# An eight-stage network on one core: table lookup of the last feed forward in parts on GpSimd beside five earlier stages, turned maxima in another bank, transposes moved in the 32-wide attentions

## The chip, the cores and the metric

One core of one Trainium2 chip. The metric is the device time of one execution in microseconds. The kernel has four batches of 512 rows of 512 float32 values and eight stages, four attentions and four feed forwards. The engines are named as in the profile: PE is TensorE, DVE is VectorE, ACT is ScalarE, POOL is GpSimd, SP is SyncE.

## What is computed

```
x = L0_attn_x                                  # (4, 512, 512)
x = x + attention(layernorm(x))                # a0: 16 heads of 32, 4 key/value heads, causal
x = x + feed_forward(layernorm(x), scales)     # f0: silu(x g) * (x u) through 1408, scaled
x = x + attention(layernorm(x), biases)        # a1: 16 heads of 32, own layernorm inside
x = x + mixture_of_depths(layernorm(x))        # m1: 64 of 512 rows are chosen
x = x + attention(layernorm(x), rope, biases)  # a2: one head of 512
x = x + ternary_feed_forward(layernorm(x))     # f2
x = x + window_attention(layernorm(x))         # a3: 16 heads of 128, window of 128
# f3: the weights are given as indices into a table of 16 values
gate, up = x @ lut[gate_idx].T, x @ lut[up_idx].T     # 1376 x 512 each
x = x + (silu(gate) * up) @ lut[down_idx].T
```

The indices are int32, laid out by the host as 11 groups of 3 matrices of 128x512 (`f3_idx`). `lut[idx]` must give the exact float32 value.

## The kernel before

Every stage is one `nc.Block` or more, with a program for each engine, and a barrier of all engines at its end: no instruction of a stage starts before all engines have ended the one before. The stages and their stretches of the profiled span are a0 16.5 to 531.0, f0 to 914.6, a1 to 1487.2, m1 in two blocks to 1621.2 and 1930.9, a2 to 2260.4, f2 to 2698.3, a3 to 3568.5 (with a short block to 2770.2 ahead), the table block of f3 to 3840.8, and f3 itself to 4222.0. Activations x stay in SBUF. Nearly every product is done as three matmuls on a high and a low part of both operands (`product`, L95 to L97), so each weight and each activation is split: ACT or POOL makes the high part (`_hi`), DVE or POOL subtracts it (`_lo`).

In the attentions an `ORDER` list, written out in Python, gives the order of work; each engine walks through all of it and does its own share of each entry, waiting on semaphores. PSUM has 8 banks; `jobs` says which job uses which bank, and `vacant`, `full` and `read` are the waits that come with it.

- **attention32** (a0, a1). A batch b has four units u of four heads. "max" computes scores for the row maxima (banks 0 to 2, DVE reduces them in L595), "rows" turns the negated maxima (`L`) on PE (L725) and ACT copies them to `mrow` (L514); "exp" computes transposed scores with the maxima added (banks 3 to 5), ACT does the exponential (L523) into `PT`; "pv" sums, "bc" spreads the reciprocals, DVE multiplies into `OT_raw` (L628), and in a0 POOL splits it (L471, L473). At the end of a batch stand "T" (PE transposes the next batch's xn, ACT evicts, POOL casts in L456, DVE subtracts in L560), "pv" of the last unit, "qkv" of the next batch, and "Y". The turned maxima use bank 0. There are 64 "exp" entries in each stage.
- **feed_forward** (f0, f3). For each batch, 11 chunks j: PE does gate and up of chunk j + 1, then down of chunk j. ACT applies silu, DVE multiplies by up (`sg`), and POOL makes `h_hi` (L1008) and `h_lo` (L1010), for which PE waits before down. In batch 0 ACT and DVE also split the weights, four chunks ahead (L1020, L1075). The next batch is normalised at j = 6 into four `xn` buffers (L1063) and turned on PE (`turn`, L1124) before the last down. SP issues three small loads and 11 weight loads at the start (L977 to L982).
- **the table block of f3** (lines 871 to 933). SP loads the indices, DVE takes the four bits of each index, ACT makes for each of 8 pairs of table values the one that the lowest bit chooses, in the eight banks, and DVE's copy_predicated picks by the other bits, then splits into `W[0]` and `W[1]`. PE and POOL have no work in it. f3 itself then loads and splits nothing.
- **mixture_of_depths** (m1). In its first block POOL does only the roots of each batch (L2296, L2297) between DVE's statistics (L2326, L2329) and DVE's normalisation (L2335); DVE's further chain of a batch follows. SP issues 13 loads, the last four of 2 MB each (L2286).
- **attention512** (a2). POOL multiplies by cosines ("qk", L1300, `by_cos`), which the rotation on DVE needs (L1433) before ACT and DVE split Q and K (L1319, L1400); PE's first "S" of a batch waits for all eight. At "U" POOL adds the output bias to x (L1306, `x_res`) and does the next batch's roots (L1288, L1290). At "S", "PT" and "PV" it has nothing to do. There are 48 such entries.

## Time and profile before

| | us |
|---|---|
| median of 3 runs (4225.61 to 4227.09) | 4226.6 |
| the profiled execution | 4223.76 |
| its span | 4222.0 |

| engine | busy us | share of the span |
|---|---|---|
| PE | 3286.4 | 78% |
| PE weight load (beside PE) | 2457.6 | 58% |
| DVE | 1948.2 | 46% |
| ACT | 1125.1 | 27% |
| POOL | 571.0 | 14% |

The mean granted TensorE clock is 0.874 of full speed. Shares are averages over stages with different limits; a stage has to be read by itself, with the views of the span in stretches, of one engine's instructions in time, and of the waits.

### The profile page before, as it was taken

The page shows a single profiled execution, that of the slowest core. Times are in us where ns is not written, and L with a number is a line of the kernel's source. Part 1 is how long each engine was busy: PE and PEld are TensorE (multiplying, and loading weights), DVE is VectorE, ACT ScalarE, POOL GpSimd, SP SyncE. Part 2 cuts the span into 40 slices and gives each one's busy share as a digit, 9 for nine tenths or more (in the row PEclk, how much of TensorE's full clock was granted, in tenths as well). Part 3 has the DMA queues.
Part 4 walks back from the last instruction along what each step waited for, and adds up shares of the span by engine and source line. Part 5 has one row for each costly group of instructions (what it writes and reads, how often), then busy time and mean ns, then how long its engine had stood idle before and what let it go on. Part 6 is the DMA issues. An engine that isn't in the chain of part 4 may idle for free. (4 is left out here: it accounts for less than half of the span.)

```text
span 4222.0 us, 52847 instructions
## 1 busy us (share of the span) xinstructions
PE 3286.4 (78%) x19938; PEld 2457.6 (58%) x19938; DVE 1948.2 (46%) x4076; ACT 1125.1 (27%) x2319; POOL 571.0 (14%) x713
## 2 busy tenths in 40 slices
PE   6889999988999948787883688859697877005999
PEld 5667678866667624464772566536565655004887
DVE  3343332223333354206676665456465555895111
ACT  2223221012223201202220222124343434673000
POOL 0011032220110000001220000012122121001222
PEclk8898899998999968898996889979898989557999
DMA  2000020010000021121002000200000001000000
GB/s 71 1 2 1 2 85 1 1 46 1 1 1 2 1 102 40 40 80 45 1 1 80 1 0 0 83 18 1 1 1 1 1 1 65 17 0 0 11 11 20
DMA packets 44823, 88.48 MB, mean 21 GB/s; under 512 B 6691, under 2 KB 10275, under 8 KB 43941
## 3 DMA queue, kind: packets, MB, share of 16 engines
q1 hardware_dynamic: 44166, 85.08, 5.7%
q8 instruction: 162, 2.65, 0.3%
q14 instruction: 79, 0.65, 0.0%
q0 software_dynamic: 416, 0.10, 0.0%
HBM read 81.07 MB, written 4.19 MB: 20 GB/s over the span
## 5 line engine op out<-in xcount | busy, mean ns | idle before, releaser
L595 DVE TENSOR_REDUCE a_nm<-bank 128x1 f32<-128x384 f32 (+3 forms) x512 | 215.4, 483 | 231.0 <-PE bank L714 230.8
L95 PE MATMUL bank<-f_xT_hi,f_w_hi 128*128 128x512 f32 (+1 forms) x704 | 275.4, 391 | 5.7 <-DVE f_w_lo L1075 4.0
L96 PE MATMUL bank<-f_xT_hi,f_w_lo 128*128 128x512 f32 (+1 forms) x704 | 275.0, 391 | 0.0
L97 PE MATMUL bank<-f_xT_lo,f_w_hi 128*128 128x512 f32 (+1 forms) x704 | 274.9, 391 | 0.0
L523 ACT ACTIVATE a_PT<-bank 128x512 f32<-128x512 f32 (+1 forms) x384 | 174.4, 526 | 321.1 <-PE bank L717 321.1
L1124 PE MATMUL bank<-ident,f_xn 128*128 128x128 f32 x128 | 18.5, 307 | 284.3 <-DVE f_xn L1063 284.3
L891 ACT ACTIVATE bank<-f_bit,f_lut,f_step 128x512 f32<-128x512 int32 x264 | 190.9, 767 | 87.3 <-DVE bank L928 47.7
L1124 PEld LDWEIGHTS bank<-ident,f_xn 128*128 128x128 f32 x128 | 17.2, 161 | 286.0 <-DVE f_xn L1063 285.2
L1095 DVE TENSOR_TENSOR f_sg<-bank,f_sg 128x512 f32<-128x512 f32 (+1 forms) x44 | 30.4, 691 | 285.2 <-PE bank L97 285.2
L2169 PE MATMUL bank<-a_KT,a_QT 128*128 128x256 f32 (+1 forms) x512 | 141.4, 385 | 19.8 <-ACT a_QT L1966 19.8
L1093 DVE SCALAR_TENSOR_TENSOR f_sg<-bank,f_us,f_sg 128x512 f32<-128x512 f32 x44 | 33.0, 750 | 264.3 <-PE bank L97 264.3
L928 DVE COPY_PREDICATED bank<-f_bit,bank 128x512 f32<-128x512 int32 x231 | 147.8, 689 | 13.1 <-DVE bank L928 4.1
L95 PEld LDWEIGHTS bank<-f_xT_hi,f_w_hi 128*128 128x128 f32 (+1 forms) x704 | 132.0, 187 | 34.7 <-issue 6.2
L96 PEld LDWEIGHTS bank<-f_xT_hi,f_w_lo 128*128 128x128 f32 (+1 forms) x704 | 132.0, 188 | 28.6
L97 PEld LDWEIGHTS bank<-f_xT_lo,f_w_hi 128*128 128x128 f32 (+1 forms) x704 | 131.9, 187 | 28.7
L1976 ACT ACTIVATE a_P<-bank,a_nm,a_qs 128x256 f32<-128x256 f32 (+1 forms) x256 | 134.0, 540 | 21.2 <-DVE a_nm L2072 21.2
L1008 POOL CAST f_h_hi<-f_sg 128x512 fp32r<-128x512 f32 (+1 forms) x88 | 65.3, 742 | 547.0 <-DVE f_sg L1095 276.0
L95 PE MATMUL bank<-f_w_hi,f_h_hi 128*128 128x512 f32 (+1 forms) x352 | 137.7, 391 | 0.2 <-POOL f_h_lo L1010 0.2
L97 PE MATMUL bank<-f_w_lo,f_h_hi 128*128 128x512 f32 (+1 forms) x352 | 137.0, 389 | 0.0
L96 PE MATMUL bank<-f_w_hi,f_h_lo 128*128 128x512 f32 (+1 forms) x352 | 137.0, 389 | 0.0
L1987 ACT ACTIVATE a_PT<-bank 128x512 f32<-128x512 f32 x112 | 61.6, 595 | 245.8 <-PE bank L2180 245.8
L2062 DVE TENSOR_REDUCE a_mx<-bank 128x2 f32<-128x512 f32 (+1 forms) x128 | 79.2, 624 | 87.5 <-PE bank L2171 87.4
(442 smaller groups left out, 8398.3 us busy)
## 6 DMA issues: line engine op xcount, KB each, us to landing
...
m_piece<-in_m_wq SPq DMA_DIRECT2D x2, 2048.0 KB, 12.3
m_piece<-in_m_wo SPq DMA_DIRECT2D x2, 2048.0 KB, 8.4
m_piece<-in_m_w_gate SPq DMA_DIRECT2D x2, 2048.0 KB, 10.8
m_piece<-in_m_w_up SPq DMA_DIRECT2D x2, 2048.0 KB, 8.1
m_piece<-in_m_w_down SPq DMA_DIRECT2D x2, 2048.0 KB, 10.7
```

The source lines that it names most:

```text
L95: pe.matmul(out, w[0], x[0], start=first, stop=False, skip_group_check=True)
L96: pe.matmul(out, w[1], x[0], start=False, stop=False, skip_group_check=True)
L97: return pe.matmul(out, w[0], x[1], start=False, stop=last, skip_group_check=True)
L523: act.activation(PT[j][:, g, :], ps[J.bank(key)][:, 0:WIDTH[j]], ACT.Exp, scale=scale).then_inc(J.frees(key), 1)
L595: last = dve.tensor_reduce(nm[:, qt, g:g + 1], ps[J.bank(key)][:, col:col + (qt + 1) * P], AX.X, ALU.max, negate=True)
L891: act.activation(ps[k][:, :], bit[ring][0][:, :], ACT.Identity, bias=lut[:, 2 * k:2 * k + 1], scale=step[:, k:k + 1]).then_inc(ones_ready. ...
L928: dve.copy_predicated(ps[keep][:, :], bit[ring][by][:, :], ps[other][:, :]).then_inc(picks.sem, 1)
L1008: pool.tensor_copy(h[i % 2][0][0:n, :], sg[i % 2][0:n, :]).then_inc(c_hi.sem, 1)
L1976: e = act.activation(Pr[i][:, hh, lo:2 * P], ps[3 + j][:, s * 2 * P + lo:(s + 1) * 2 * P], ACT.Exp, bias=small["nm"][:, i, hh:hh + 1], sca ...
L1987: act.activation(PT[g % 2][:, j, :], ps[5 + j][:, :], ACT.Copy).then_inc(J.frees(("PT", g, j)), 1)
L2062: last = dve.tensor_reduce(small["mx"][:, i, 2 * j:2 * j + 2], ps[3 + j][:, :].rearrange("p (h n) -> p h n", h=2)[:, :, lo:2 * P], AX.X, A ...
L2169: pe.matmul(ps[3 + j][:, s * 2 * P + lo:(s + 1) * 2 * P], QT[i][:, hh * P:(hh + 1) * P], KT[:, k0:(tt + 1) * P], start=True, stop=False, s ...
```

## The change

The table block goes. Its work is done on POOL beside a0, f0, a1, m1 and a2, and the looked-up weights go to a scratch tensor in DRAM (`table_w`), from which f3 loads and splits them as f0 does. The work is cut into 66 parts of 128x256 indices. A part has 31 steps: for each of 16 values one tensor_scalar (is_equal to k, times the value k, which is read from SBUF by partition) and 15 additions in between, exact since all terms but one are zero. a0 has 14 parts, f0 16, a1 16, m1 4, a2 16. The steps of a stage are spread evenly over calls: one at each "exp" in a0 and a1, one behind each `h_lo` in f0, one behind each roots in m1, one at each "S", "PT" and "PV" in a2. A call waits for no entry of its stage, only for its own indices and steps. SP gets a list of moves behind the stage's own loads (`table_moves`): the 16 values, two parts of indices, then each finished part out and the next but one in, and at the end of the stage a wait for the last two. `begin` makes POOL wait for the 16 values: behind roots(0) in a0, f0 and a1, behind roots(0) and the constants in a2, and ahead of roots(0) in m1.

In attention32 the four "T" of the next batch move from the end of the batch to behind the four "exp" steps of its last unit, into banks 0 to 2, and the turned maxima use bank 3 instead of 0. To make room in SBUF, V has one buffer instead of two, and f0 has two xn buffers instead of four: turns 2 and 3 of a batch are normalised after the last chunk, when turns 0 and 1 are done. f3 keeps four.

```diff
@@ -31,6 +31,10 @@
 NT = NB * TT
 NEG = -3.0e38
 SLOTS = 64
+SBUF_END = 229368
+TABLE_COLS = 256
+TABLE_STEPS = 31
+TABLE_PARTS = 66
...
+        self.table_w = nc.dram_tensor("table_w", ins["f3_idx"].shape, F32).ap()
+        n, at = TABLE_COLS * 4, SBUF_END // 32 * 32 - 7 * TABLE_COLS * 4 - 64
+        self.table_idx = [self.sb(f"table_idx{i}", [P, TABLE_COLS], I32, offset=at + i * n) for i in range(2)]
+        self.table_term = [self.sb(f"table_term{i}", [P, TABLE_COLS], F32, offset=at + (2 + i) * n) for i in range(3)]
+        self.table_sum = [self.sb(f"table_sum{i}", [P, TABLE_COLS], F32, offset=at + (5 + i) * n) for i in range(2)]
+        self.table_lut = self.sb("table_lut", [P, 16], F32, offset=at + 7 * n)
+        self.table_step, self.table_lut_in = Count(self.sem("table_step")), Count(self.sem("table_lut_in"))
+        self.table_in = [Count(self.sem(f"table_in{i}")) for i in range(2)]
+        self.table_out = [Count(self.sem(f"table_out{i}")) for i in range(2)]
     def still(self, engine):
...
+def table_part(array, i):
+    part = array[i // 2 // 3][i // 2 % 3]
+    return part[:, i % 2 * TABLE_COLS:(i % 2 + 1) * TABLE_COLS]
+
+
+def table_moves(prog, sp, first, last):
+
+    def fetch(i):
+        if i >= last:
+            return
+        if i >= 2:
+            sp.wait_ge(*prog.table_step(0, (i - 2) * TABLE_STEPS + TABLE_STEPS - 2))
+        sp.dma_start(prog.table_idx[i % 2][:, :], table_part(prog.ins["f3_idx"], i)).then_inc(prog.table_in[i % 2].sem, 16)
+
+    sp.dma_start(prog.table_lut[:, :], prog.ins["f3_lut"].partition_broadcast(P)).then_inc(prog.table_lut_in.sem, 16)
+    fetch(first)
+    fetch(first + 1)
+    for i in range(first, last):
+        sp.wait_ge(*prog.table_step(0, (i + 1) * TABLE_STEPS))
+        sp.dma_start(table_part(prog.table_w, i), prog.table_sum[i % 2][:, :]).then_inc(prog.table_out[i % 2].sem, 16)
+        fetch(i + 2)
+    for i in (last - 2, last - 1):
+        sp.wait_ge(*prog.table_out[i % 2](0, 16 * (i // 2 + 1)))
+
+
+def table_steps(prog, pool, start, end):
+
+    for n in range(start, end):
+        i, s = n // TABLE_STEPS, n % TABLE_STEPS
+        idx, total = prog.table_idx[i % 2], prog.table_sum[i % 2]
+        if s == 0:
+            pool.wait_ge(*prog.table_in[i % 2](0, 16 * (i // 2 + 1)))
+            if i >= 2:
+                pool.wait_ge(*prog.table_out[i % 2](0, 16 * (i // 2)))
+            pool.tensor_scalar(total[:, :], idx[:, :], 0.0, prog.table_lut[:, 0:1], ALU.is_equal, ALU.mult).then_inc(prog.table_step.sem, 1)
+        elif s == 1 or s % 2 == 0 and s < TABLE_STEPS - 1:
+            k = 1 if s == 1 else s // 2 + 1
+            if n >= 3:
+                pool.wait_ge(*prog.table_step(0, n - 2))
+            pool.tensor_scalar(prog.table_term[k % 3][:, :], idx[:, :], float(k), prog.table_lut[:, k:k + 1], ALU.is_equal,
+                               ALU.mult).then_inc(prog.table_step.sem, 1)
+        else:
+            k = 15 if s == TABLE_STEPS - 1 else (s - 1) // 2
+            pool.wait_ge(*prog.table_step(0, n if k == 15 else n - 1))
+            pool.tensor_tensor(total[:, :], total[:, :], prog.table_term[k % 3][:, :], ALU.add).then_inc(prog.table_step.sem, 1)
+
+
+class TableShare:
+
+
+    def __init__(self, prog, parts, calls):
+        self.prog, self.first, self.last, self.calls, self.n = prog, parts[0], parts[1], calls, 0
+
+    def begin(self, pool, stage):
+        pool.wait_ge(*self.prog.table_lut_in(0, 16 * stage))
+
+    def run(self, pool):
+        a, total = self.first * TABLE_STEPS, (self.last - self.first) * TABLE_STEPS
+        table_steps(self.prog, pool, a + self.n * total // self.calls, a + (self.n + 1) * total // self.calls)
+        self.n += 1
+
...
@@ -356,11 +431,13 @@
                     ORDER.append(("bc", (b, u - 1), 0))
                 if k >= 2:
                     ORDER.append(("pv", (b, u), k - 2))
+                if u + 1 == DC and b + 1 < NB:
+                    ORDER.append(("T", b + 1, k))
             if u + 1 < DC:
                 ORDER.append(("rows", (b, u + 1), 0))
         end = (b, DC - 1)
         if b + 1 < NB:
-            ORDER += [("T", b + 1, c) for c in range(DC)] + [("pv", end, 2)]
+            ORDER.append(("pv", end, 2))
             ORDER += [("qkv", b + 1, i) for i in range(len(QKV))] + [("bc", end, 0)]
             for k in range(4):
                 ORDER += [("Y", b, k), ("max", (b + 1, 0), k)]
@@ -371,14 +448,14 @@
     jobs = [("const", 7)] if biased else []
     for kind, at, k in ORDER:
         if kind == "T":
-            jobs.append(((kind, at, k), k))
+            jobs.append(((kind, at, k), k if at == 0 else MAX_BANK + k % 3))
         elif kind == "qkv":
             jobs.append(((kind, at, k), (k + 4) % 6))
         elif kind in ("max", "exp"):
             base = MAX_BANK if kind == "max" else EXP_BANK
             jobs += [((kind, at, f), base + f % 3) for f in range(3 * k, 3 * k + 3)]
         elif kind == "rows":
-            jobs.append(((kind, at), MAX_BANK))
+            jobs.append(((kind, at), EXP_BANK))
         elif kind == "pv" and k == 0:
             jobs += [(("O", at), O_BANK), (("sum", at), SUM_BANK)]
         elif kind == "bc":
@@ -421,6 +498,7 @@
                         sp.dma_start(bv[:, :], ins[f"{name}_bv"]).then_inc(c_const.sem, 16)
             if biased:
                 sp.dma_start(bo[:, :], ins[f"{name}_bo"].partition_broadcast(P)).then_inc(w_in[3].sem, 16)
+            table_moves(prog, sp, *share)
         @block.gpsimd
         def _(pool):
@@ -450,8 +528,12 @@
                 pool.tensor_tensor(prog.rstd[:, r], var[:, 1, r], var[:, 2, r], ALU.mult).then_inc(c_rstd.sem, 1)
             roots(0)
+            table = TableShare(prog, share, len([1 for e in ORDER if e[0] == "exp"]))
+            table.begin(pool, 1 if split_y else 3)
             for kind, at, k in ORDER:
-                if kind == "T":
+                if kind == "exp":
+                    table.run(pool)
+                elif kind == "T":
                     pool.wait_ge(*read((kind, at, k)))
                     pool.tensor_copy(xT[0][:, k, :], xT_raw[:, k, :]).then_inc(c_xhi.sem, 1)
                 elif kind == "rows" and at[1] == 1 and at[0] + 1 < NB:
@@ -499,7 +581,7 @@
                     key, (what, c) = (kind, at, k), QKV[k]
                     act.wait_ge(*full(key))
                     if what == "V":
-                        act.activation(V[at % 2][:, c, :], ps[J.bank(key)][:, 0:KC * P], ACT.Copy).then_inc(J.frees(key), 1)
+                        act.activation(V[:, c, :], ps[J.bank(key)][:, 0:KC * P], ACT.Copy).then_inc(J.frees(key), 1)
                         continue
                     to = (Q if what == "Q" else K)[0][:, c, :]
                     if biased:
...
-    xn = [prog.sb(f"{name}_xn{i}", [P, D], F32) for i in range(TT)]
+    NX = 2 if share else TT
+    xn = [prog.sb(f"{name}_xn{i}", [P, D], F32) for i in range(NX)]
...
-    if table:
-        N_PIECES = NJ * 3
...
-                pick(N_PIECES - 1, 0)
...
-            if not table:
-                for j in range(NJ):
-                    sp.dma_start(W_raw[:, j * 3 * D:(j + 1) * 3 * D].rearrange("p (m d) -> p m d", m=3),
-                                 ins[f"{name}_w"][j].rearrange("m p d -> p m d")).then_inc(w_in[j].sem, 16)
+            if not share:
+                for i in range(2):
+                    sp.wait_ge(*prog.table_out[i](0, 16 * TABLE_PARTS // 2))
+            for j in range(NJ):
+                sp.dma_start(W_raw[:, j * 3 * D:(j + 1) * 3 * D].rearrange("p (m d) -> p m d", m=3),
+                             weights[j].rearrange("m p d -> p m d")).then_inc(w_in[j].sem, 16)
...
+            if share:
+                table = TableShare(prog, share, NB * NJ)
+                table.begin(pool, 2)
...
+                    if share:
+                        table.run(pool)
...
-            def normalise(b):
+            def normalise(b, which):
                 dve.wait_ge(*c_rstd(0, b + 1))
-                for tt in range(TT):
+                for tt in which:
                     t = b * TT + tt
-                    if b:
+                    if b and NX == TT:
                         dve.wait_ge(*full("T", b - 1, tt))
-                    dve.tensor_scalar(xn[tt][:, :], x[:, t * D:(t + 1) * D], prog.mv[:, t, 0:1], prog.rstd[:, t:t + 1],
+                    elif tt >= NX:
+                        dve.wait_ge(*full("T", b, tt - NX))
+                    elif b:
+                        dve.wait_ge(*full("T", b - 1, tt + NX))
+                    dve.tensor_scalar(xn[tt % NX][:, :], x[:, t * D:(t + 1) * D], prog.mv[:, t, 0:1], prog.rstd[:, t:t + 1],
                                       ALU.subtract, ALU.mult).then_inc(c_xn.sem, 1)
...
                     if j == 6 and b + 1 < NB:
-                        normalise(b + 1)
+                        normalise(b + 1, range(NX))
                 if b + 1 < NB:
+                    if NX < TT:
+                        normalise(b + 1, range(NX, TT))
                     rest(b + 1)
...
+            table = TableShare(prog, share, 3 * NT)
+            table.begin(pool, 5)
             for kind, b, k in ORDER:
-                if kind == "qk":
+                if kind in ("S", "PT", "PV"):
+                    table.run(pool)
...
         def _(pool):
+            table = TableShare(prog, share, NB)
+            table.begin(pool, 4)
             for b in range(NB):
                 v = prog.var
...
                 pool.tensor_tensor(prog.rstd[:, 0:TT], v[:, 0, 0:TT], prog.mhalf[:, 0:TT], ALU.pow).then_inc(stats_c[2].sem, 1)
+                table.run(pool)
...
-        attention32(prog, "a0", 1, False)
-        feed_forward(prog, "f0", 1408, True, False, False)
-        attention32(prog, "a1", DC, True)
-        mixture_of_depths(prog, "m1")
-        attention512(prog, "a2")
+        attention32(prog, "a0", 1, False, (0, 14))
+        feed_forward(prog, "f0", 1408, True, False, (14, 30))
+        attention32(prog, "a1", DC, True, (30, 46))
+        mixture_of_depths(prog, "m1", (46, 50))
+        attention512(prog, "a2", (50, 66))
         ternary_feed_forward(prog, "f2")
         window_attention(prog, "a3")
-        feed_forward(prog, "f3", 1376, False, True, True)
+        feed_forward(prog, "f3", 1376, False, True, None)
 def kernel(**inputs):
```

What is left out is the body of the table block, the same for `weight`, `gate_up` and `turn` (they lose the case of a looked-up table, and index xn by tt % NX), the counters at the end of each stage, and the calls of `table_moves` in f0, m1 and a2, which stand last in SP's list of loads.

## Rows read from the trace of the kernel before

The columns of groups and instructions are the line of the kernel, engine, operation, output and inputs, shapes and count, then busy us, mean ns of one, and idle time of the engine before them with what ended it. Instructions in time begin with their start and duration in us.

**Rows 1.** the span cut into stages: stretch, length, busy time (instructions) by engine, PEclk, DMA

```profile
16.50:531.00 514.50, 453.28 (x4976) 347.47 (x4976) 203.37 (x424) 135.89 (x282) 48.35 (x57) 0.88 0.02 7
...
531.00:914.60 383.60, 370.98 (x1648) 307.34 (x1648) 103.44 (x151) 55.53 (x72) 99.22 (x96) 0.98 0.07 24
...
914.60:1487.20 572.60, 513.38 (x5064) 371.63 (x5064) 218.40 (x440) 154.79 (x293) 48.40 (x61) 0.90 0.03 10
...
1487.20:1621.20 134.00, 56.88 (x168) 39.69 (x168) 74.76 (x209) 6.42 (x12) 5.07 (x8) 0.61 0.23 81
...
1930.90:2260.40 329.50, 266.85 (x1152) 213.46 (x1152) 216.24 (x284) 89.70 (x155) 74.40 (x56) 0.90 0.04 15
...
3568.50:3840.80 272.30, 0.00 (x0) 0.00 (x0) 236.58 (x430) 190.86 (x264) 0.00 (x0) 0.50 0.09 32
```

**Rows 2.** GpSimd's groups of instructions by line and form, with mean ns of one

```profile
L1010 POOL TENSOR_TENSOR f_h_lo<-f_sg,f_h_hi 128x512 fp32r<-128x512 f32 x84 | 108.6, 1293 | 6.7
...
L471 POOL CAST a_OT_hi<-a_OT_raw 128x512 fp32r<-128x512 f32 x16 | 9.8, 612 | 336.5 <-DVE a_OT_raw L628 336.5
...
L447 POOL TENSOR_TENSOR var<-var,mv 128x4 f32<-128x4 f32 x4 | 0.8, 202 | 0.3
...
L1936 POOL TENSOR_SCALAR a_ms<-a_ssq 128x4 f32<-128x4 f32 x64 | 12.4, 194 | 58.6 <-DVE a_ssq L2056 58.6
...
L448 POOL TENSOR_SCALAR var<-var 128x4 f32<-128x4 f32 x4 | 0.9, 230 | 0.3
...
L236 POOL TENSOR_SCALAR var<-var 128x16 f32<-128x16 f32 x1 | 0.3, 266 | 0.1
```

**Rows 3.** instructions of a2 in time, GpSimd: start, us, what, idle before

```profile
2008.67 5.06 POOL L1306 TENSOR_TENSOR x_res<-x_res,a_bo 128x512 f32<-128x512 f32 x4 [32.41 <-ACT a_bo L1355]
...
2047.83 1.79 POOL L1300 TENSOR_TENSOR a_by_cos<-a_flat,a_trig 128x512 f32<-128x512 f32 x1 [28.83 <-ACT a_flat L1339]
...
2120.53 1.79 POOL L1300 TENSOR_TENSOR a_by_cos<-a_flat,a_trig 128x512 f32<-128x512 f32 x1 [32.52 <-ACT a_flat L1339]
...
2218.20 6.72 POOL L1306 TENSOR_TENSOR x_res<-x_res,a_bo 128x512 f32<-128x512 f32 x4
```

**Rows 4.** instructions of f0 in time, GpSimd

```profile
552.79 2.06 POOL L1008 CAST f_h_hi<-f_sg 128x512 fp32r<-128x512 f32 x1 [17.37 <-DVE f_sg L1093]
...
615.28 0.61 POOL L1008 CAST f_h_hi<-f_sg 128x512 fp32r<-128x512 f32 x1 [6.19 <-DVE f_sg L1093]
```

**Rows 5.** a DMA of m1 (us to landing; issue), ACT in f0, GpSimd in m1 and a0

```profile
m_piece<-in_m_wv SPq DMA_DIRECT2D x1, 2048.0 KB, 21.8
...
1497.55 3.08 SPq L2286 DMA_DIRECT2D m_piece<-in_m_wv  x1
...
545.31 1.49 ACT L1020 ACTIVATE f_w_hi<-f_w_raw 128x1536 fp32r<-128x1536 f32 x1 [0.56 <-DMA f_w_raw<-in_f_w]
...
1502.09 0.23 POOL L2296 TENSOR_SCALAR var<-mv 128x4 f32<-128x4 f32 x1 [161.42 <-DVE mv L2329]
...
24.15 0.61 POOL L456 CAST a_xT_hi<-a_xT_raw 128x512 fp32r<-128x512 f32 x1 [3.18 <-ACT a_xT_raw L494]
```

**Rows 6.** one DVE line of a2: duration ns min/median/max

```profile
L1400 DVE TENSOR_TENSOR a_KT_lo<-a_KT_raw,a_KT_hi x16: 691/1658/1707, 1971.4 to 2226.8; 128x512 fp32r<-128x512 f32 x16
```

**Rows 7.** waits in a0: engine line, what released it, us in total, times, longest

```profile
PE bank L95 <- DVE a_xT_lo L560: 8.3, 3, 2.8
PE bank L702 <- ACT a_mrow L514: 8.2, 12, 0.7
```

**Rows 8.** instructions of a0 in time, GpSimd: the end of one batch's attention

```profile
257.46 0.61 POOL L471 CAST a_OT_hi<-a_OT_raw 128x512 fp32r<-128x512 f32 x1 [13.77 <-DVE a_OT_raw L628]
...
264.98 3.20 POOL L456 CAST a_xT_hi<-a_xT_raw 128x512 fp32r<-128x512 f32 x4 [5.55 <-ACT a_xT_raw L494]
```

**Rows 9.** first products of f0 and of f3 on PE

```profile
543.48 0.77 PE L95 MATMUL bank<-f_xT_hi,f_w_hi 128*128 128x512 f32 x1 [4.05 <-DVE f_w_lo L1075]
...
3851.19 0.47 PE L95 MATMUL bank<-f_xT_hi,f_w_hi 128*128 128x512 f32 x1 [1.61 <-DVE f_xT_lo L1069]
```

121 lines of the change are left out of this document (23 added, 98 removed).

## The prediction

> **What bounds the kernel now.** I read the span cut at the barriers between the stages first, since no work crosses them: each stage can be costed alone, and the end moves by the sum [rows 1]. Everywhere but in the table stage and the first part of m1, TensorE is busy for most of the stretch, and GpSimd for little of it. The table stage (3568.5 to 3840.8) is 272.3 us in which TensorE does nothing, DVE and ACT alternating. The second reading is GpSimd's groups by form, for what one instruction of each kind costs [rows 2]. The third is GpSimd in order of time, stage by stage. There it is the idle time *at the places where the new calls stand* that counts, not the idle share: GpSimd works its list strictly in order, so an instruction put before an urgent one delays it, and idle time elsewhere in the stage is worth nothing.
>
> The sum is made against the profiled execution, 4223.8 us with a span of 4222.0. The median of the runs shown is 4226.6, 2.8 above it. A measurement of this kernel can tell about 0.2% from no change (8.5 us).
>
> **The removed part.** The table stage goes whole: -272.3 us [rows 1]. No other stage touches what it made, so nothing hides behind it.
>
> **The price of a step.** The lookup becomes 66 parts of 31 instructions on 128x256: 16 compare-and-multiply and 15 adds, 2046 in all. An add of 512 columns follows the next at 5.06/4 = 1.26 us [rows 3], 1.29 in f0; one of 4 columns takes 0.20 [rows 2]. So 256 columns need 0.20 + 252 x (1.27 - 0.20)/508 = 0.73; back to back I take 0.71. The compare-and-multiply is not in the trace at this width. From below: a cast of 512 columns, also one input, takes 0.612, and the two-operation form of tensor_scalar has a fixed part of 0.19 (0.194 at 4 columns) [rows 2]; that gives 0.19 + 252 x 0.42/508 = 0.40. From above: the one-operation form goes from 0.230 at 4 columns to 0.266 at 16 [rows 2], 3 ns a column, which carried on gives 0.23 + 252 x 0.003 = 0.99. I take 0.40, because the new instruction shares its two operations with the 0.194 row and the cast is the only one-input row of real width. A step is then (16 x 0.40 + 15 x 0.71)/31 = 0.55 us, a part 17.1 us.
>
> **a2 (16 parts, 496 steps in 48 calls).** All calls stand at S, PT and PV, between the roots of the next batch and its first by_cos. 12 calls a batch are 124 steps, 68 us. The gap there is 28.8 us in batch 0, 32.5 in batches 1 and 2 [rows 3], and after the last shift (2224.9) 35.5 us until the stage ends: 129 us of room for 273. The next by_cos waits, rotation, the low half of Q and K and then the first S with it, so the excess is serial: 144 us. I add 8 for table steps that meet DVE's normalisation (an estimate, 0 to 15), and 2 for the last part's way out. **+154.** What was late in other queues is only early by then: TensorE can run ahead by four projections, which DVE does not follow faster.
>
> **f0 (16 parts, 44 calls).** A call is 11.3 steps, 6.2 us; the gap before each cast of h is 6.19 us in the steady state [rows 4]. It just fits, with nothing to spare. What doesn't fit: in batch 0 seven casts take 2.06 instead of 0.61, behind DVE's weight split (7 x 1.45 = 10); roots and blocked steps are about 3.3 a batch (13, an estimate); TensorE's own lead of about 2.7 absorbs some. With two xn buffers instead of four, turns 2 and 3 wait for DVE, about 1 us in three places. +21 together (10 to 30). Then a queue: begin() makes GpSimd wait for the 16-value table, whose DMA stands on SP's queue behind all 11 weight loads. ACT got the fourth load as it landed at 545.3; at about 2.1 us each (at most 2.4: the stage's DMA share, 0.07 of 383.6 us, over 11 loads [rows 1]) the eleventh lands near 560, while GpSimd's first cast now runs at 552.8 [rows 4, 5]. +7. **+28.**
>
> **m1 (4 parts, one call a batch).** Here begin() stands before the first roots. Its DMA is behind four loads of 2 MB and nine small ones; the last of them is issued at 1497.55 and lands 21.8 later, at 1519.4, while roots now start at 1502.1 and DVE waits for them [rows 5]. **+18** (0 if transfers overtake). After roots, a 17 us call runs beside a DVE chain with two-input operations. What such a meeting costs is seen in a2: DVE's subtraction of two SBUF tensors takes 0.69 us alone and up to 1.71 beside a GpSimd multiply (median 1.66), blocked for the rest of the other's run [rows 6]. About 16 operations a batch meet a step of 0.40 or 0.71: between 0 and 9 us a batch, I take 6: **+24**. I expect the last call to end inside the stage.
>
> **a0 and a1.** Two gains. TensorE waits for the eviction of turned maxima 12 times, 8.2 us in a0; in another bank that wait falls under the next maxima. It waits 8.3 us in three places for xT_lo at the end of a batch [rows 7]; with the transposes spread over the last unit this should fall to nothing. Against it: in a0 a call is 6.8 steps, 3.7 us, so four calls and the two OT operations need 16.9 us of GpSimd per unit, while the gaps before OT_hi are 13.8 to 15.6 us plus 1.9 of its own work. So in the last unit GpSimd arrives late: from OT_hi of the third unit (257.5, already about 1.5 late) it still has two to three calls between the four casts and ends near 273, where the casts ended at 268.2 [rows 8]. That is +5 a batch, not -2.8. a0: 3 x 5 - 8 + 4 for the table value's DMA ahead of the first cast at 24.15 [rows 5] (0 to 4) = **+12**. a1 has no OT work on GpSimd, which gets ahead, and the casts are only about 1 us a batch late: 3 - 8 = **-5**. For both together -30 to +40.
>
> **f3.** It now loads and splits weights as f0 does: its first product comes 12.4 us after the barrier (543.48 - 531.06) instead of 10.3 (3851.19 - 3840.84) [rows 9]. **+2.** The scratch in DRAM is written long before; that wait is free.
>
> **Sum.** -272 + 154 + 28 + 18 + 24 + 12 - 5 + 2 = -39. 4223.8 - 39 = 4185, and against the median 4188; I say **4186**.
>
> **How firm.** The price of the compare-and-multiply decides. In a2 and in f0 there are 256 of them each on the path; with those of a0, a1 and m1 that count, 0.1 us more costs about 64 us. No change comes at 0.46 us.
>
> **Rivals.**
> *The middle price (slower).* In f0 and a2 the same mechanism, GpSimd as the bound, but with a compare-and-multiply between a cast (0.40) and a two-input add (0.71), say 0.55. It decides from 0.46 on. 0.15 x 640 = +96: 4282, and at 0.71 about 4385. For it: compare, multiply, and conversion from integers are more than a cast does. Against: the two-operation row at 4 columns shows no extra time.
> The Trainium skill, GPSIMD Engine Reference, section "Elementwise — side-by-side cycle accounting", gives about 1.8 cycles an element, 769 ns for 512 elements, as the best of a tight loop; an estimate from that page is 0.48 us for 256, which would make the whole about 4237; no row here shows it.
> *The slow path.* 3 ns a column as in the one-operation rows, 0.99 us: +378, 4563, with a0 and a1 saturated as well. For it: two rows with the same slope. Against: they are another form, of few columns.
> *The late work is hidden.* a2's excess is not serial, because engines that ran ahead catch up, or the parts' instructions overlap more than the 1.26 us pitch of adds says, and the reordering in a0 and a1 gives its 16 us in each. 4110 to 4140, say 4125. Against: every rotation needs its by_cos, and the gaps above are all the room that GpSimd has for the calls.
> *The gains and costs cancel* within 8 us.
>
> **Chances.** Forecast 0.50 (its own range 4150 to 4222), middle price 0.25, slow path 0.12, hidden 0.08, cancel 0.05. Faster by over 0.2%: 0.08 and most of the 0.50, 0.54. Within: 0.06. Slower: 0.40. The range takes in all but the slow path and the end of the hidden case: 4130 to 4390.
>
> **What would show it.** Right: no instructions between a3 and f3; compare-and-multiply near 0.40 and adds near 0.71 us; a2 near 483 us with GpSimd busy nearly throughout its attention phases and by_cos the releaser of DVE's longest waits; f0 near 411 with the first cast of h near 560; m1's first part near 176, its first roots near 1520 relative to now; a0 and a1 within some 15 us of before. Wrong: a2 near 330, a compare-and-multiply over 0.46, or a0 and a1 well shorter.

## The result, and the profile after

The changed kernel takes 4832.5 us (median of 4 runs, 4826.6 to 4841.5), against 4226.9 us of the kernel before: 1.143 times as long (95% interval 1.141 to 1.145). 4186 was forecast, in a range of 4130 to 4390. The change costs 606 us. The profiled execution has a span of 4829.7 us, 607.7 above that of before.

First the changed kernel cut at its barriers, as [rows 1] show the kernel before. The columns are: stretch, its length, busy time (instructions) of PE, PE weight load, DVE, ACT and POOL, the granted clock, the DMA share and GB/s.

```profile
16.30:652.80 636.50, 448.97 (x4976) 343.89 (x4976) 207.57 (x424) 136.91 (x282) 461.74 (x491) 0.82 0.04 12
652.80:1282.50 629.70, 443.74 (x1648) 346.93 (x1648) 104.41 (x151) 56.23 (x72) 558.95 (x592) 0.86 0.06 21
1282.50:1935.30 652.80, 520.57 (x5064) 376.46 (x5064) 222.67 (x440) 155.46 (x293) 519.85 (x557) 0.84 0.05 15
1935.30:2113.90 178.60, 56.76 (x168) 39.71 (x168) 88.13 (x209) 6.42 (x12) 134.18 (x132) 0.59 0.19 66
2430.30:3132.10 701.80, 273.69 (x1152) 217.99 (x1152) 215.91 (x284) 89.34 (x155) 538.06 (x552) 0.69 0.04 13
```

They are a0, f0, a1, the first part of m1 and a2. GpSimd, busy for 48 of 514.5 us in a0 before, is now busy for 462 of 636.5, and for 559 of 629.7 in f0.

| stage | before | forecast | measured | difference measured |
|---|---|---|---|---|
| a0 | 514.5 | +12 | 636.5 | +122.0 |
| f0 | 383.6 | +28 | 629.7 | +246.1 |
| a1 | 572.6 | -5 | 652.8 | +80.2 |
| m1, first part | 134.0 | +42 | 178.6 | +44.6 |
| a2 | 329.5 | +154 | 701.8 | +372.3 |
| table | 272.3 | -272 | gone | -272.3 |
| f3 | 381.1 | +2 | 386.1 | +5.0 |

Stages with unchanged code make the remaining 10 us: m1's second part +6.7, a3 +3.4. Over all profiles in which their code is that of before, these two came out at 306 to 317 and 795 to 802 us, with no edit to explain it. Differences of a few microseconds in a single profile are left uninterpreted.

Next the two costliest of GpSimd's groups of instructions in the changed kernel: busy us, mean ns of one, idle time before them.

```profile
L329 POOL TENSOR_SCALAR table_term<-table_idx,table_lut 128x256 f32<-128x256 int32 x990 | 1158.3, 1171 | 79.8
L334 POOL TENSOR_TENSOR table_sum<-table_sum,table_term 128x256 f32<-128x256 f32 x990 | 726.4, 734 | 65.5
```

The add has the 0.73 us that was worked out for it from [rows 2, 3]. The compare-and-multiply has 1.17 us where 0.40 was taken. And there is idle time ahead of the steps, 0.07 to 0.08 us each on average. It shows in order of time, here in f0 between two casts of h (start, us, instruction):

```profile
904.47 1.22 POOL L329 TENSOR_SCALAR table_term<-table_idx,table_lut 128x256 f32<-128x256 int32 x1
905.75 0.68 POOL L1002 CAST f_h_hi<-f_sg 128x512 fp32r<-128x512 f32 x1
906.51 1.26 POOL L1004 TENSOR_TENSOR f_h_lo<-f_sg,f_h_hi 128x512 fp32r<-128x512 f32 x1
907.74 0.73 POOL L334 TENSOR_TENSOR table_sum<-table_sum,table_term 128x256 f32<-128x256 f32 x1
908.57 1.16 POOL L329 TENSOR_SCALAR table_term<-table_idx,table_lut 128x256 f32<-128x256 int32 x1
909.80 0.73 POOL L334 TENSOR_TENSOR table_sum<-table_sum,table_term 128x256 f32<-128x256 f32 x1
```

From one add to the next, 907.74 to 909.80, a pair of steps takes 2.06 us; the forecast had 0.40 + 0.71 = 1.11.

The idle time is not ahead of every step. Here the beginning of a part in a2 (its first step, at 2518.59, is not shown; x2 are two steps in one row):

```profile
2519.85 2.27 POOL L329 TENSOR_SCALAR table_term<-table_idx,table_lut 128x256 f32<-128x256 int32 x2
2522.08 0.74 POOL L334 TENSOR_TENSOR table_sum<-table_sum,table_term 128x256 f32<-128x256 f32 x1
2522.80 1.14 POOL L329 TENSOR_SCALAR table_term<-table_idx,table_lut 128x256 f32<-128x256 int32 x1
2523.91 0.73 POOL L334 TENSOR_TENSOR table_sum<-table_sum,table_term 128x256 f32<-128x256 f32 x1
2524.74 1.14 POOL L329 TENSOR_SCALAR table_term<-table_idx,table_lut 128x256 f32<-128x256 int32 x1
```

The third to the sixth step each begin 0.01 to 0.04 us before the record of the one ahead ends; the seventh, at 2524.74, begins 0.10 after it. It is so in all 66 parts wherever two steps stand side by side: no gap ahead of the third to the sixth step, and from the seventh on 0.10 us ahead of a compare-and-multiply and 0.08 ahead of an add.

### The profile page after: what moved, and what is told of

Same layout as the page of the kernel before. It is cut to its first block and busy times, and to the rows that moved or that the text cites. A ratio compares the mean times of both kernels' runs of the same rounds, so it can differ in the third digit from the quotient of the medians.

```text
span 4829.7 us, 53485 instructions
## 1 busy us (share of the span) xinstructions
PE 3381.8 (70%) x19938; PEld 2511.8 (52%) x19938; DVE 1753.2 (36%) x3657; ACT 951.0 (20%) x2066; POOL 2517.7 (52%) x2759
## 5 line engine op out<-in xcount | busy, mean ns | idle before, releaser
L329 POOL TENSOR_SCALAR table_term<-table_idx,table_lut 128x256 f32<-128x256 int32 x990 | 1158.3, 1171 | 79.8
L334 POOL TENSOR_TENSOR table_sum<-table_sum,table_term 128x256 f32<-128x256 f32 x990 | 726.4, 734 | 65.5
L99 PE MATMUL bank<-f_w_hi,f_h_hi 128*128 128x512 f32 (+1 forms) x352 | 165.6, 470 | 166.5 <-POOL f_h_lo L1004 166.5
L99 PE MATMUL bank<-a_xT_hi,a_wk_hi 128*128 128x512 f32 x144 | 59.8, 416 | 276.4 <-ACT a_flat L1345 273.4
L1939 POOL TENSOR_TENSOR a_sq<-a_q 128x512 f32<-128x512 f32 x64 | 66.5, 1040 | 326.5 <-DVE a_q L2058 326.5
L99 PEld LDWEIGHTS bank<-f_w_hi,f_h_hi 128*128 128x128 f32 (+1 forms) x352 | 78.4, 223 | 200.3 <-POOL f_h_lo L1004 183.7
L99 PEld LDWEIGHTS bank<-a_xT_hi,a_wk_hi 128*128 128x128 f32 x144 | 28.5, 198 | 286.3 <-ACT a_flat L1345 274.6
L99 PE MATMUL bank<-a_xT_hi,a_wq_hi 128*128 128x512 f32 x192 | 83.7, 436 | 123.9 <-DVE a_xT_lo L642 99.1
L824 PE MATMUL bank<-a_PT,a_V 128*32 128x512 f32 (+3 forms) x1024 | 100.1, 488 | 98.7 <-issue 98.7
L100 PE MATMUL bank<-f_w_hi,f_h_lo 128*128 128x512 f32 (+1 forms) x352 | 159.3, 452 | 0.0
L100 PEld LDWEIGHTS bank<-f_xT_hi,f_w_lo 128*128 128x128 f32 (+1 forms) x704 | 134.0, 190 | 29.6
```

What stands on the lines that cost most here:

```text
L99: pe.matmul(out, w[0], x[0], start=first, stop=False, skip_group_check=True)
L100: pe.matmul(out, w[1], x[0], start=False, stop=False, skip_group_check=True)
L329: pool.tensor_scalar(prog.table_term[k % 3][:, :], idx[:, :], float(k), prog.table_lut[:, k:k + 1], ALU.is_equal, ALU.mult).then_inc(prog. ...
L334: pool.tensor_tensor(total[:, :], total[:, :], prog.table_term[k % 3][:, :], ALU.add).then_inc(prog.table_step.sem, 1)
L824: last = pe.matmul(ps[J.bank(key)][strip, kt * P:T], v, PT[k][:, g, col:col + (TT - kt) * P], start=kt == 0, stop=kt == 2, skip_group_chec ...
L1939: pool.tensor_tensor(sq[:, :], q[i][:, :], q[i][:, :], ALU.mult).then_inc(c["q_sq"].sem, 1)
```

## The experiments

The lengths of the stages in each profile (us) are what most readings below rest on. "Steps" says what GpSimd executes in the place of the lookup, "placed" and "even" how its calls are weighted. Each row is one profile.

| kernel | steps | a0 | f0 | a1 | m1, 1st | a2 | table | f3 | span |
|---|---|---|---|---|---|---|---|---|---|
| before | none | 514.5 | 383.6 | 572.6 | 134.0 | 329.5 | 272.3 | 381.1 | 4222.0 |
| after | 66 parts | 636.5 | 629.7 | 652.8 | 178.6 | 701.8 | - | 386.1 | 4829.7 |
| e2_cast_price | 66, cast | 556.3 | 401.8 | 577.1 | 168.5 | 460.3 | - | 386.0 | 4183.1 |
| e6_one_operation | 66, one multiply | 599.7 | 555.2 | 608.0 | 167.7 | 623.3 | - | 386.1 | 4581.4 |
| e3_no_steps | none | 495.2 | 394.0 | 557.8 | 150.8 | 329.4 | - | 385.9 | 3951.2 |
| e4_order_only | none | 488.8 | 383.1 | 551.5 | 133.7 | 329.5 | 270.3 | 380.8 | 4168.7 |
| e5_bank_only | none | 504.1 | 383.4 | 564.3 | 132.7 | 329.5 | 270.4 | 382.9 | 4204.0 |
| e7_mixed | 30, placed | 494.8 | 389.6 | 548.7 | 134.2 | 329.4 | 145.6 | 384.0 | 4064.2 |
| e8_even | 30, even | 558.1 | 391.8 | 590.6 | 132.8 | 329.4 | 145.5 | 384.0 | 4168.7 |
| e9_more | 42, placed | 494.0 | 393.3 | 551.7 | 131.9 | 329.2 | 99.5 | 383.0 | 4033.6 |

**What makes the compare-and-multiply slow.** The theory was the form itself; the rivals were its integer input, the comparison, and the company of VectorE. The kernel before gets a block at its end in which GpSimd works alone, six times each of 13 forms, each waiting for the one ahead. Five of them:

```diff
+            for r in range(R):
+                go(pool.tensor_scalar(yf[:, 0:256], xi[:, 0:256], 3.0, tab[:, 3:4], ALU.is_equal, ALU.mult))
+            for r in range(R):
+                go(pool.tensor_scalar(yf[:, 0:256], xf[:, 0:256], 3.0, tab[:, 3:4], ALU.is_equal, ALU.mult))
+            for r in range(R):
+                go(pool.tensor_scalar(yf[:, 0:256], xf[:, 0:256], 3.0, 0.5, ALU.is_equal, ALU.mult))
+            for r in range(R):
+                go(pool.tensor_scalar(yf[:, 0:256], xf[:, 0:256], 3.0, 0.5, ALU.mult, ALU.add))
+            for r in range(R):
+                go(pool.tensor_scalar(yf[:, 0:256], xf[:, 0:256], 3.0, None, ALU.mult))
```

> The kernel before with a block added behind the last stage, in which GpSimd alone runs 13 forms of instruction six times each, one after the other. In the changed kernel the compare-and-multiply took 1.14 us at 256 columns where I had 0.40. Theory 'form': the whole tensor_scalar path costs some 4 ns a column once it is wide, whatever the input type: then f32 input and immediates are about 1.1 us too, multiply-and-add as well, 128 columns about 0.66, 512 about 2.1. Theory 'integers': the int32 input is what costs, then f32 input gives about 0.4 and an int32 cast is near 1 us. Theory 'compare': is_equal costs, then multiply-and-add on f32 is about 0.4 and the compare stays near 1.1 with f32. Theory 'meeting DVE': DVE is idle here, so each would be about 0.4, and the 1.14 comes from blocked ports; its minimum of 1.132 in the changed kernel speaks against it. The add on 256 columns 0.73 by all.

The kernel with that block takes 4294.7 us (one run). Most groups of the block follow. The lines in question are L2835, L2837 and L2839 (the form of the change at 128, 256 and 512 columns), L2841 (input in float32), L2843 (both scalars written into the instruction), L2845 (multiply, add), L2847 (one multiply), L2849 (multiply, add) and L2851 (compare, multiply) on 4 columns:

```profile
L2839 POOL TENSOR_SCALAR pr_yf<-pr_xi,pr_tab 128x512 f32<-128x512 int32 x6 | 12.0, 1994 | 0.6
L2837 POOL TENSOR_SCALAR pr_yf<-pr_xi,pr_tab 128x256 f32<-128x256 int32 x6 | 6.8, 1141 | 0.6
L2841 POOL TENSOR_SCALAR pr_yf<-pr_xf,pr_tab 128x256 f32<-128x256 f32 x6 | 6.8, 1141 | 0.6
L2843 POOL TENSOR_SCALAR pr_yf<-pr_xf 128x256 f32<-128x256 f32 x6 | 6.4, 1067 | 0.5
L2847 POOL TENSOR_SCALAR pr_yf<-pr_xf 128x256 f32<-128x256 f32 x6 | 5.1, 850 | 0.5
...
L2835 POOL TENSOR_SCALAR pr_yf<-pr_xi,pr_tab 128x128 f32<-128x128 int32 x6 | 4.3, 720 | 0.6
...
L2845 POOL TENSOR_SCALAR pr_yf<-pr_xf 128x256 f32<-128x256 f32 x6 | 2.4, 406 | 0.5
L2831 POOL CAST pr_yf<-pr_xi 128x256 f32<-128x256 int32 x6 | 2.4, 400 | 0.4
...
L2851 POOL TENSOR_SCALAR pr_yf<-pr_xf 128x4 f32<-128x4 f32 x6 | 1.4, 232 | 0.5
L2849 POOL TENSOR_SCALAR pr_yf<-pr_xf 128x4 f32<-128x4 f32 x6 | 1.2, 194 | 0.5
```

Integer or float input makes no difference (1141 and 1141 ns), the pointer costs 74 ns, and with VectorE idle it is as slow as beside it (1.14 alone, 1.17 in the kernel). It is which operations the instruction has: multiply-and-add takes 0.406 us, as long as a cast (0.400), and compare-and-multiply with the same kinds of operands takes 1.067. Even a single multiply takes 0.850, so the comparison alone is not what is slow. The slope from 128 to 512 columns is (1.994 - 0.720)/384 = 3.3 ns a column, against (0.612 - 0.400)/256 = 0.8 for the cast. On 4 columns the quick pair takes 194 ns and the slow one 232; a single multiply was not run at that width.

**Whether that price is the whole cause.** The changed kernel with a cast in the place of each compare-and-multiply; waits, order and count of steps stay. The lookup is left out, so f3's weights are not the looked-up ones.

```diff
-            pool.tensor_scalar(prog.table_term[k % 3][:, :], idx[:, :], float(k), prog.table_lut[:, k:k + 1], ALU.is_equal,
-                               ALU.mult).then_inc(prog.table_step.sem, 1)
+            pool.tensor_copy(prog.table_term[k % 3][:, :], idx[:, :]).then_inc(prog.table_step.sem, 1)
```

> The changed kernel with each compare-and-multiply replaced by a cast of the same indices to f32 (the lookup is left out: its output is not the weights). All waits, calls and DMAs stay. Theory 'price alone': if 0.40 against 1.14 us is all that was wrong, the time is what I forecast, 4186 within 40: a2 483, f0 411, m1's first part 176, a0 527, a1 568. Rival 'more than the price': calls in the way of urgent work, lost overlap or blocked DVE cost more than the sum says: over 4260 even at this price. Rival 'clock': idle gaps lower the granted clock in stages that the change leaves alone; then m1's second part and a3 are again 7 and 4 us longer than before.

It took 4184.9 us (one run), against the 4186 of the forecast, though not by the stages expected: a0 came to 556.3 for 527, a2 to 460.3 for 483. GpSimd's groups in it, and the same kind of stretch as above in order of time:

```profile
L333 POOL TENSOR_TENSOR table_sum<-table_sum,table_term 128x256 f32<-128x256 f32 x990 | 753.7, 761 | 5.2
L329 POOL CAST table_term<-table_idx 128x256 f32<-128x256 int32 x990 | 431.8, 440 | 0.0
```

```profile
801.88 0.74 POOL L333 TENSOR_TENSOR table_sum<-table_sum,table_term 128x256 f32<-128x256 f32 x1
802.57 0.40 POOL L329 CAST table_term<-table_idx 128x256 f32<-128x256 int32 x1
802.92 0.74 POOL L333 TENSOR_TENSOR table_sum<-table_sum,table_term 128x256 f32<-128x256 f32 x1
```

A pair takes 1.04 us here: the next instruction begins 0.05 us before the record of the last one ends. In the changed kernel's rows in f0 it begins 0.06 to 0.11 after that end, but for the add behind h_lo. So 0.77 us of price (1.17 - 0.40; 0.73 by the mean of 0.44 here) became 1.02 us a pair, and 646.6 us of span for 1.02 us is 634 us for 1 us of pair, beside the forecast's slope of 640.

**Whether the time rises evenly with it.** The same with one multiply by a constant (again the lookup is left out), whose price lies between:

```diff
-            pool.tensor_scalar(prog.table_term[k % 3][:, :], idx[:, :], float(k), prog.table_lut[:, k:k + 1], ALU.is_equal,
-                               ALU.mult).then_inc(prog.table_step.sem, 1)
+            pool.tensor_scalar(prog.table_term[k % 3][:, :], idx[:, :], float(k), None, ALU.mult).then_inc(prog.table_step.sem, 1)
```

> The kernel after, with each compare-and-multiply of 256 columns replaced by one multiply by a constant (the lookup itself is left out). Measured alone this form takes 0.85 us, between the cast (0.40 alone, 0.43 in the kernel) and the compare-and-multiply (1.14 alone, 1.17 in the kernel). If the price of one instruction is all there is to it, and the time rises evenly with it, the span lies on the line between those two kernels: 4183 + (0.88 - 0.43)/0.74 x 646 = 4576 us, a0 near 605, f0 near 540, a2 near 605 us. If the forecast's slope of 640 us for 1 us holds up to where GpSimd becomes the bound of a0, f0, a1 and m1 and the rest comes only beyond that, it is 4183 + 0.45 x 640 = 4471 us. If something else than the price of the instruction held the kernel after (the comparison's reading of integers, the pointer to a scalar), the span stays near 4250 us.

4583.2 us (one run), 7 from the straight line in the price of an instruction and 112 above the other count. Here the gaps are there too: adds follow each other at 1.75 us (799.71, 801.46), though 0.85 + 0.73 is 1.58. The time rises with price and gap, with an instruction that reads no pointer and compares nothing; a2 is at 623.3, f0 at 555.2, 18 and 15 above what was expected of them. In the pitch of a pair it doesn't rise evenly: 398.3 us of span for the first 0.71 us (1.04 to 1.75), 561 for 1 us, and 248.3 for the next 0.31, 801 for 1 us. The 634 above is the mean of two slopes, and that it meets the 640 is in part chance.

```profile
799.71 0.73 POOL L333 TENSOR_TENSOR table_sum<-table_sum,table_term 128x256 f32<-128x256 f32 x1
800.53 0.85 POOL L329 TENSOR_SCALAR table_term<-table_idx 128x256 f32<-128x256 int32 x1
801.46 0.73 POOL L333 TENSOR_TENSOR table_sum<-table_sum,table_term 128x256 f32<-128x256 f32 x1
```

**What the change costs and gains without its steps.** The waits for the 16 values, the order, the single V, the two xn and f3's loads stay; steps and moves of indices go. f3 computes with f0's weights in the place of the looked-up ones.

```diff
     sp.dma_start(prog.table_lut[:, :], prog.ins["f3_lut"].partition_broadcast(P)).then_inc(prog.table_lut_in.sem, 16)
-    fetch(first)
-    fetch(first + 1)
...
     def run(self, pool):
-        a, total = self.first * TABLE_STEPS, (self.last - self.first) * TABLE_STEPS
-        table_steps(self.prog, pool, a + self.n * total // self.calls, a + (self.n + 1) * total // self.calls)
```

> The changed kernel without the 2046 steps, their index loads and stores (left out: the lookup; f3 uses other weights of the same shape in their place). The waits for the 16 values, the moved transposes, the other bank, the single V, the two xn buffers and f3's own weight loads stay. Theory 'steps': nearly all of the loss is in the steps, so this is 4222 - 272 + 18 (m1) + 7 + 3 (f0) + 5 (a0, a1 values) - 33 (moved transposes, bank) + 4 (f3) = about 3954, a0 about 502, a1 about 556, a2 330, f0 394. Rival 'other parts': the moved transposes or the single V or xn pair cost tens of us by themselves: over 4000.

3953.0 us (one run), as expected. f0 is 10.4 and the first part of m1 16.8 us longer than before without one step. In m1 that is the wait for the 16 values behind the loads on SP's queue; in f0 it is the same wait and the two xn buffers. In the changed kernel the waits stand as GpSimd's in f0 and m1 (start, us, instruction, idle before it):

```profile
682.77 0.61 POOL L1002 CAST f_h_hi<-f_sg 128x512 fp32r<-128x512 f32 x1 [25.52 <-DMA table_lut<-in_f_lut]
```

```profile
1967.72 0.23 POOL L2305 TENSOR_SCALAR var<-mv 128x4 f32<-128x4 f32 x1 [50.17 <-DMA table_lut<-in_f_lut]
```

The cast comes 30.0 us after f0's barrier (21.8 before, [rows 4]), the roots of m1 32.4 after theirs (14.9 before, [rows 5]).

**The order in the 32-wide attentions alone**, applied to the kernel before:

```diff
+                if u + 1 == DC and b + 1 < NB:
+                    ORDER.append(("T", b + 1, k))
...
-            ORDER += [("T", b + 1, c) for c in range(DC)] + [("pv", end, 2)]
+            ORDER.append(("pv", end, 2))
...
-            jobs.append(((kind, at, k), k))
+            jobs.append(((kind, at, k), k if at == 0 else MAX_BANK + k % 3))
...
-            jobs.append(((kind, at), MAX_BANK))
+            jobs.append(((kind, at), EXP_BANK))
```

> The kernel before with only the reordering of the 32-wide attentions: transposes of the next batch behind the exp steps of the last unit in banks 0 to 2, turned maxima in bank 3. Table block and everything else as before. My forecast's terms without GpSimd in the way: 8 us in each of a0 and a1 from the bank and 8 to 13 in each from the transposes, so 4190 to 4197, ratio 0.992. Rival 'hidden': the waits move to the next resource (ACT in the last unit), then under 8 us in all, ratio over 0.998.

4176.3 us (4 runs), 0.989 of before (0.987 to 0.991): more than was expected (4190 to 4197), 25.7 us in a0 and 21.1 in a1, where the forecast had 16 in each.

**Its bank alone.** Only the last of these edits:

> The kernel before with one word changed: the turned maxima of the two 32-wide attentions go to the bank of the exponentials. The transposes stay where they were. If the bank is what counts, the waits of VectorE for the rows of maxima (8.2 us a unit in the kernel before, 2.9 us with both edits) fall as with both edits, 5 us in each of 4 units, and most of the 25.7 and 21.1 us that both edits took out of the two stages is here: a0 about 490 us. If the place of the transposes is what counts (the waits for the turned queries and keys fell from 8.3 to 3.3 us and that for the turned probabilities went), the bank alone gives 5 to 10 us a stage at most, a0 505 to 510 us and a1 563 to 568 us, and a time of 4206 to 4217 us. I take the second.

What was expected misread one row: the 8.2 us are TensorE's, not VectorE's, over all 12 waits of a0 and not per unit [rows 7]; the 2.9 us stand at another line (2.7 us in the kernel before).

4202.7 us (4 runs), 0.994 (0.992 to 0.995), 3 below the range expected; a0 loses 10.4 us, a1 8.3. The larger part, 15.3 and 12.8 us, comes with the transposes. TensorE's waits in a0 (in total, times, longest), first of the bank alone, then of both edits:

```profile
PE bank L95 <- DVE a_xT_lo L560: 8.3, 3, 2.8
PE bank L702 <- DVE a_nm L595: 8.1, 5, 1.9
...
PE bank L706 <- ACT a_PT L523: 5.1, 8, 0.7
```

```profile
PE bank L704 <- DVE a_nm L597: 5.3, 3, 2.0
...
PE bank L95 <- DVE a_xT_lo L562: 3.3, 3, 1.1
PE bank L708 <- ACT a_mrow L516: 2.9, 4, 0.7
PE bank L708 <- ACT a_PT L525: 1.7, 5, 0.7
```

The bank takes away the 12 waits for mrow (8.2 us, [rows 7]), but those for nm, the row maxima, rise from 5.2 us to 8.1: 5.3 us net, where a0 lost 10.4. The transposes take away 5.0 us of xT_lo, 3.4 for PT and 2.8 for nm: 11.2 us of 15.3. Where the rest went was not traced.

**A version that gains.** What the runs said so far: steps cost little where GpSimd is idle at their place; a2 and the first part of m1 have few such places, f0 has some; the reordering gains by itself. So 30 of the 66 parts go to GpSimd, in a0, f0 and a1 only, the calls weighted into idle stretches, no step in the last unit of a batch but the fourth; the 16 values are loaded once; VectorE and ScalarE make the other 6 of 11 pieces in the table's stage.

```diff
-        attention32(prog, "a0", 1, False, (0, 14))
-        feed_forward(prog, "f0", 1408, True, False, (14, 30))
-        attention32(prog, "a1", DC, True, (30, 46))
-        mixture_of_depths(prog, "m1", (46, 50))
-        attention512(prog, "a2", (50, 66))
+        attention32(prog, "a0", 1, False, (0, 10))
+        feed_forward(prog, "f0", 1408, True, False, False, (10, 17))
+        attention32(prog, "a1", DC, True, (17, 30))
+        mixture_of_depths(prog, "m1")
+        attention512(prog, "a2")
...
+                    if u == 0:
+                        return 50
+                    if u == 1:
+                        return (125, 125, 35, 35)[k]
+                    if u == 2:
+                        return (35, 35, 40, 40)[k]
+                    return 0 if b + 1 < NB else (30, 30, 0, 0)[k]
```

> A version meant to gain from what the runs showed. The kernel before, with the order and the bank of the changed kernel (4176 us by itself), and with 30 of the 66 parts on GpSimd, in a0, f0 and a1 alone: 10, 7 and 13 parts, the calls weighted into the stretches where the trace of before has GpSimd idle, none ahead of the last unit of a batch. VectorE and ScalarE still make 6 of the 11 pieces of the table in their own stage, which falls from 265 to about 145 us. A part costs 30.5 us of GpSimd at the slow price: 305 us in a0 where GpSimd is idle for over 300 us of 489, 214 us in f0, 397 us in a1. If idle time of GpSimd costs nothing where the steps lie in it, the time is 4176 - 120 + 10 = 4066 us. If a step delays whatever instruction follows it (half a step, 0.5 us, for each of some 300 handovers) and GpSimd's share is too large, the three stages grow by 60 us or more and it comes to about 4120 us. If they grow by over 120 us, the version loses to the reordering alone (4176).

4062.0 us (5 runs; 4066 expected), 0.960 of before (0.959 to 0.962). GpSimd's steps in a0, 300 us of them, cost 6.0 us against the reordering alone (494.8 against 488.8), in f0 6.5, and a1 got 2.8 us shorter.

**The same parts, placed evenly.**

```diff
-            table = TableShare(prog, share, [weight_of(*e) for e in ORDER if e[0] in ("qkv", "exp")])
+            table = TableShare(prog, share, [1 for e in ORDER if e[0] == "exp"])
```

f0's calls, nearly even before, are made equal too.

> The mixed version again, with the same 30 parts in the same three stages (10 in a0, 7 in f0, 13 in a1), but the steps dealt out evenly over the calls ahead of the turned weights, as the changed kernel does it, where the mixed version puts more of them where GpSimd is idle and none in the last unit of a batch. If the place of the steps counts, the splits of the attention's output in the last unit wait again: in the changed kernel PE waited 43.4 us in 4 for them in a0, and a0 there stood 148 us above the reordered kernel for 14 parts. I expect 15 to 40 us more in each of a0 and a1, little in f0, and a time of 4095 to 4140 us. If only the amount of work on GpSimd counts, it is 4062 us again.

4176.3 us (4 runs), 0.988 (0.986 to 0.989): above the 4095 to 4140 expected. a0 is 63.3 and a1 41.9 us longer than with the placed steps; the same work on the same engine in the same stages then gains nothing over the reordering alone (spans 4168.7 in both). TensorE's waits in a0, even and then placed:

```profile
PE bank L100 <- DVE a_xT_lo L644: 30.9, 3, 10.3
PE bank L100 <- POOL a_OT_lo L557: 24.5, 4, 15.3
```

```profile
PE bank L100 <- POOL a_OT_lo L575: 12.1, 4, 3.1
...
PE bank L100 <- DVE a_xT_lo L662: 3.8, 3, 1.6
```

**Carried on.** 42 parts: one more in each of a0, f0 and a1, and 9 in the second part of m1, behind its two pairs of roots, with SP's moves set between the weight loads.

```diff
+            table = TableShare(prog, share, [6, 3])
             for r in range(2):
                 pool.wait_ge(*c_ss(0, r + 1))
...
                 pool.tensor_tensor(sm[:, 2, :], sm[:, 1, :], prog.mhalf[:, 0:ST], ALU.pow).then_inc(c_rt.sem, 1)
+                table.run(pool)
```

> The mixed version carried on: 42 parts on GpSimd (11 in a0, 8 in f0, 14 in a1, and 9 in the second part of m1, where GpSimd has nothing to do for 199 and some 115 us between two calls), and 4 instead of 6 pieces made by VectorE and ScalarE. The table's own stage falls by two pieces of 24.3 us, from 145.6 to 97 us. If the parts in m1 lie wholly in its idle time (6 x 30.3 = 182 us in 199, 3 x 30.3 = 91 us in 115) and one part more in each of the other stages costs 5 us, the time is 4062 - 49 + 15 = 4028 us. If GpSimd's share in the attentions is at its edge, a part more costs up to its whole 30 us each, and the time is 4062 - 49 + 75 = 4088 us, worse than the mixed version.

4041.0 us (5 runs), 0.955 (0.954 to 0.957), the best of these kernels that compute the network: 188 us faster than the kernel before (4229.2 beside it) and 791 faster than the changed kernel. It is 13 above the first count (4028) and 47 below the second. The table's stage fell by 46.1 us. f0 gave back 3.7, a1 3.0, m1's second part 5.9 (322.5 against 316.6), a3 7.3 with unchanged code. Such small differences of two profiles are within what a3 shows by itself.

## Why the prediction was wrong, step by step

**The price of a step** is the step that failed: 0.40 us taken for a compare-and-multiply that takes 1.17. By the forecast's own slope the 0.77 us are 493 us (an estimate), and no other step is needed to leave the range. "I take 0.40, because the new instruction shares its two operations with the 0.194 row and the cast is the only one-input row of real width". It does not share them: the 0.194 row is multiply, add, and the new instruction is compare, multiply. That a form has two operations doesn't group it; which two they are does. The bound from above, 0.99 from 3 ns a column [rows 2], came near (3.3 measured), and was set aside because the rows are "another form, of few columns", which the chosen row was as well. It rests on one pair of rows, 12 columns apart, not on two rows that agree. The 0.48 us of the middle price is not half of the 769 ns beside it either, which is 0.38; both are far under the 1.07 to 1.14 measured. With a cast in its place the total came out 1 us off (4184.9 against 4186); with the real one, 646 us off.

**The range** ended at 4390, short of the slow path that stood among the rivals with a chance of 0.12. That rival, 4563, was itself 270 us short: 0.18 us more price (1.17 against 0.99) is 115 us at its slope of 640, and 0.25 us more pair than price (1.02 against 0.77) is 160 us by the same slope; this split is an estimate. The forecast's bounds were of the instruction alone and never of the pair in sequence. What opens the gap is not settled by these runs: the casts never have it, and the slow steps have it from the seventh of a part on, but not at the third to the sixth, which are the same instructions. (The last add of a part, which waits for the one ahead, comes 0.08 us after it in every kernel.)

**a2** failed by its price only. 496 steps less 129 us of room: at 0.52 us a step (cast) this gives 129 us, measured 130.8; at 1.03 (half of 2.06) it gives 382, measured 372.3. DVE's wait for by_cos is the serial excess of three batches, as said (in total, times, longest); the fourth batch's steps run on to the end of the stage:

```profile
DVE a_QT_raw L1439 <- POOL a_by_cos L1306: 281.7, 3, 96.5
```

The 8 us added for meetings with DVE can't be seen in this sum.

**f0**: at the forecast's price it cost 18.2 us for 28 said, of which the queue and the two xn buffers 10.4 (7 and 3 said) and the steps 7.8 (18 said). At the real price a chunk is 12.9 us from cast to cast (905.75 to 918.66) where a call had to fit into a gap of 6.19 [rows 4], and TensorE waits for GpSimd in nearly every chunk:

```profile
PE bank L99 <- POOL f_h_lo L1004: 166.5, 41, 10.5
```

**m1**: the queue was right (17.5 us later roots, 18 said). Steps at the quick price cost 17.7 us for 24 said. At the real price GpSimd is the bound: its roots come 36.0 us apart (1967.72, 2003.75) for a call of 31 steps.

**a0 and a1** were mis-sized in two terms of opposite sign, at the forecast's own price. The reordering gained 25.7 and 21.1 us, not 16; waits and single V gave 6.4 and 6.3 back; the steps then cost 61.1 and 19.3 us (e2_cast_price less e3_no_steps), where 15 and 3 were said. In sum a0 was +41.8 for +12, a1 +4.5 for -5. Together with the 23 us too much in a2 and the 10 and 8 in f0 and m1, the total came right by luck: an agreement to 1 us in the total is no proof of the terms.

What the forecast missed in a0 differs with the price. At the quick price the OT splits are not late: TensorE waits 12.1 us for OT_lo in e2_cast_price, as in e3_no_steps. Its waits for xT_lo grow by 13.0 us (3.3 to 16.3), those for L, the negated maxima, by 14.7 (6.6 to 21.3), and it is busy 32 us longer (446.5 to 478.3) at a granted clock of 0.83 for 0.90; together these are about the 61.1 us. Behind the waits for L stands VectorE, held by the quick steps; in time, its cast of 16 columns, and the GpSimd rows around it:

```profile
110.87 6.82 DVE L689 CAST a_L<-a_nm 128x16 fp32r<-128x16 f32 x1 [0.20 <-DVE a_nm L676]
```

```profile
110.73 0.77 POOL L333 TENSOR_TENSOR table_sum<-table_sum,table_term 128x256 f32<-128x256 f32 x1
...
116.52 0.44 POOL L329 CAST table_term<-table_idx 128x256 f32<-128x256 int32 x1
116.88 1.62 POOL L333 TENSOR_TENSOR table_sum<-table_sum,table_term 128x256 f32<-128x256 f32 x2
```

That cast takes 0.18 us in e3_no_steps. Here it ends at 117.69, as the first add of the last row does (the second follows 0.08 us after it), 12 steps without a gap later. The 16 of them in a0 take 23.8 us for 3.0. The forecast took such a meeting to last "for the rest of the other's run", one instruction; it lasted until GpSimd paused, and so did four others of these casts, of 2.1 to 6.8 us. In the changed kernel, whose slow steps mostly stand apart, the longest is 0.68 us. So the cast is not the changed kernel with a lower price alone.

At the real price the place is what costs: e8_even against e7_mixed has 63.3 us in a0 for the same 10 parts, with TensorE's waits for both OT_lo and xT_lo; the clock may have a part in it (see the last section).

**f3** +5.0 and the table's stage -272.3 came as said, within what unchanged stages vary.
